# A macaron block with a selective scan on one core: the product of dt and u made by VectorE, two units later, in place of GpSimd

## What is computed

```python
x = x + 0.5 * ffn(layernorm(x))
x = x + attn(layernorm(x))          # its norm has a weight and a bias; attn adds its input too
x = x + 0.5 * ffn(layernorm(x))

# attn, per sequence: 512 channels d, 64 states s
x_ssm, z = split(h @ Win)
u  = silu(conv4(x_ssm) + conv_b)
dt = softplus(u @ dt_w + dt_b)
B, C = u @ Bp, u @ Cp
state = state * exp(dt * A) + (dt * u)[:, None] * B      # for each token in turn
y = einsum(state, C) + u * D
out = x + (y * silu(z)) @ Wout
```

## Time and profile before

| | |
|---|---|
| median of 3 runs | 5663.76 us (5656.84 to 5670.63) |
| profiled execution | 5668.32 us, its span 5666.1 us |
| granted TensorE clock | 0.972 of full speed |
| GpSimd busy | 5087.2 us, 90% of the span, 2326 instructions |
| VectorE busy | 5003.5 us, 88%, 4659 instructions |
| TensorE matmul busy | 4967.1 us, 88%, 85192 instructions |
| ScalarE busy | 3993.9 us, 70% |

### The profile page before, as it was taken

The page is one execution under the profiler, slowest core; times in us unless marked ns, Lnnn a source line. Parts: engine busy times, 40 slices in busy tenths (PEclk is TensorE's granted clock), DMA queues, the critical chain, the costliest instruction groups (busy, mean ns, idle before and its releaser), DMA issues.

```text
span 5666.1 us, 203628 instructions
## 1 busy us (share of the span) xinstructions
PE 4967.1 (88%) x85192; PEld 3086.8 (54%) x85192; DVE 5003.5 (88%) x4659; ACT 3993.9 (70%) x6625; POOL 5087.2 (90%) x2326
## 2 busy tenths in 40 slices
PE   4798988989889898998989889898898989889887
PEld 1455555555555555555555555555555555555554
DVE  1699989899998999989989898998989999898996
ACT  3677776777767677686767777777776777767564
POOL 0699898999989899898998989999899998989996
PEclk9899999999999999999999999999999999999998
DMA  5475565656547565565655656565475655646553
GB/s 159 146 172 189 152 182 173 168 191 157 188 162 176 181 167 184 164 173 181 169 189 152 180 180 170 188 167 186 159 178 184 172 187 158 180 169 176 193 181 114
DMA packets 578970, 977.29 MB, mean 172 GB/s; under 512 B 294881, under 2 KB 328450, under 8 KB 510466
## 3 DMA queue, kind: packets, MB, share of 16 engines
q1 hardware_dynamic: 313858, 961.82, 54.5%
q10 hardware_dynamic: 264192, 2.11, 3.0%
HBM read 875.74 MB, written 88.08 MB: 170 GB/s over the span
## 4 chain that ended last, share of the span: by engine, by line
POOL 57%; issue 25%; PE 10%; DVE 3%; DMA 2%; ACT 1%; POOLq 1%; ACTq 0%; DVEq 0%; SPq 0%
POOL H L625 54%; PE pUB L701 3%; PE Y L727 3%; DVE H L586 2%; PE pP L664 1%; POOL lnv L639 1%; DMA Bd<-scratch_diag 1%; POOL dto L643 1%; PE pP L658 1%; DMA Cb<-scratch_c 1%; PE pA L743 0%; POOLq L624 0%; DVE cv L537 0%; POOL X L649 0%; PE pA L741 0%
## 5 line engine op out<-in xcount | busy, mean ns | idle before, releaser
L625 POOL TENSOR_TENSOR H<-H,Cb 128x1024 f32<-128x1024 f32 x2048 | 4801.9, 2393 | 351.7 <-DVE H L586 344.9
L586 DVE TENSOR_TENSOR_SCAN H<-dA,pUB 128x512 f32<-128x512 f32 x4096 | 4678.6, 1202 | 464.2 <-PE pUB L701 438.0
L427 ACT ACTIVATE dA<-DT,w_negA 128x512 f32<-128x512 f32 x4096 | 2620.3, 711 | 1316.0 <-DVE H L586 1311.9
L701 PEld LDWEIGHTS pUB<-Bd,UT 64*64 64x64 f32 x65536 | 1963.9, 135 | 1427.1 <-issue 1416.8
L701 PE MATMUL pUB<-Bd,UT 64*64 64x128 f32 x65536 | 2282.6, 276 | 487.5 <-DVE H L586 405.0
L727 PE MATMUL Y<-H,w_ident 64*64 64x512 f32 x16384 | 2037.2, 607 | 93.0 <-POOL H L625 92.0
L727 PEld LDWEIGHTS Y<-H,w_ident 64*64 64x64 f32 x16384 | 670.6, 137 | 679.9 <-issue 668.9
L427 ACT ACT_TABLE_LOAD x224 | 287.4, 1283 | 4.0
L658 PE MATMUL pP<-hT,w_Win 128*128 128x512 f32 x512 | 266.3, 644 | 25.7 <-ACT uto L415 15.0
L664 PE MATMUL pP<-U,w_dt_w 128*128 128x512 f32 x512 | 259.2, 631 | 4.6 <-ACT zo L379 4.6
L639 POOL TENSOR_TENSOR lnv<-lnv,ev 128x512 f32<-128x512 f32 x64 | 81.2, 1269 | 82.3 <-DVE ev L600 82.3
(11 more groups left out here) (78 smaller groups left out, 1909.5 us busy)
## 6 DMA issues: line engine op xcount, KB each, us to landing
Cb<-scratch_c SPq DMA_DIRECT2D x512, 1024.0 KB, 5.3
Bd<-scratch_diag SPq DMA_DIRECT2D x512, 512.0 KB, 4.5
scratch_diag<-H SPq DMA_DIRECT2D x16, 1024.0 KB, 18.0
scratch_z<-zo SPq DMA_DIRECT2D x64, 256.0 KB, 6.1
scratch_dt<-dto SPq DMA_DIRECT2D x64, 256.0 KB, 5.8
scratch_ut<-uto SPq DMA_DIRECT2D x64, 256.0 KB, 6.3
DT<-scratch_dt SPq DMA_DIRECT2D x64, 256.0 KB, 4.9
UT<-scratch_ut SPq DMA_DIRECT2D x64, 256.0 KB, 5.6
```

What stands on the lines that cost most here:

```text
L427: last = nc.scalar.activation(dA[:, n % DAR, j, :], DT[:, k, :], ACT.Exp, scale=c["negA"][:, k, GS * blk + j:GS * blk + j + 1])
L586: last = nc.vector.tensor_tensor_scan(H[:, n % HR, 2 * i + j, :], dA[:, n % DAR, 2 * i + j, :], pUB[:, i, :].rearrange("p (t s) -> p s t", ...
L625: nc.gpsimd.tensor_tensor(h[:, j:j + 2, :], h[:, j:j + 2, :], Cb[:, blk % 2, j:j + 2, :], ALU.mult).then_inc(times_c, 1)
L701: last = nc.tensor.matmul(out, UT[rows, k, j * P + h * HP:j * P + h * HP + HP], Bd[rows, blk % 2, i, j * P:(j + 1) * P].rearrange("p (t s) ...
```

## The change

The product leaves GpSimd's dt step and becomes an instruction of VectorE behind its scans of unit 32, 37, 44 and 51, two units after the GpSimd additions of the same tile (behind unit 30, 35, 42, 49). VectorE waits for dto and for duo to be free. Nothing else is moved: the store of dto, the transposition and the tables of the other engines are as before.

```diff
-DVES = {..., "soft": (30, 35, 42, 49),
+DVES = {..., "soft": (30, 35, 42, 49), "du": (32, 37, 44, 51),
...
 # VectorE, behind the scans of unit n
+                    if proj and n in when["du"]:
+                        m = when["du"].index(n)
+                        s = KI * q + m
+                        dve.wait_ge(dt_done, at(s + 1))
+                        dve.wait_ge(mm_ut, at(s))
+                        nc.vector.tensor_tensor(duo[:, :], dto[:, :], U[:, m, :], ALU.mult).then_inc(du_done, 1)
...
 # GpSimd, behind its products of unit n
                         nc.gpsimd.tensor_tensor(dto[:, :], lnv[:, :], relu[:, :], ALU.add).then_inc(dt_done, 1)
-                        pool.wait_ge(dt_done, at(s + 1))
-                        pool.wait_ge(mm_ut, at(s))
-                        nc.gpsimd.tensor_tensor(duo[:, :], dto[:, :], U[:, m, :], ALU.mult).then_inc(du_done, 1)
```

More of the change, by code:

```diff
@@ L36 @@
         "turn 1": (18, 21), "turn c": (35, 37), "turn 3": (58, 60)}
-DVES = {"norm 1": (4,), "norm c": (21,), "norm 2": (40,), "norm 3": (52,), "soft": (30, 35, 42, 49),
+DVES = {"norm 1": (4,), "norm c": (21,), "norm 2": (40,), "norm 3": (52,), "soft": (30, 35, 42, 49), "du": (32, 37, 44, 51),
         "conv": (2, 6, 10, 14), "x2": (11, 15), "x1": (27, 32), "out": (42, 46)}
```

## The result

| | before | changed |
|---|---|---|
| median of 20 runs each | 5658.6 us (5638.8 to 5675.9) | 5674.5 us (5662.4 to 5690.3) |
| ratio | | 1.0025, 95% interval 1.0014 to 1.0035 |
| profiled execution's span | 5666.1 us | 5660.5 us |
| GpSimd busy, instructions | 5087.2 us, 2326 | 5032.8 us, 2262 |
| VectorE busy, instructions | 5003.5 us, 4659 | 5068.1 us, 4723 |

In this measurement the change costs a quarter of a percent; the forecast was 28 us less. The profiled execution of the changed kernel is the quickest of its 20 and that of before lies above its median, so the two spans say nothing of the sign. They can be compared place by place.

What follows compares the result with a forecast made beforehand. Any of GpSimd, VectorE and TensorE can bound a unit, with TensorE waiting for GpSimd behind dt steps. Gains of 1.8 us x 15 passes, 27 us, plus about 1 for q = 0, gave 5636 us; range 5595 to 5695.

Steps and rivals of the forecast that it cites:

- The port: SBUF port shared by VectorE and GpSimd: new product put at 0.67 us if free, 4 us or more if not.
- Case (b): VectorE waits only for GpSimd's running product, then goes ahead of the next; seen at 2101.09, L600 taking 2.17 us.
- (c): VectorE waits for the running GpSimd product and the whole next one; seen at unit 49, L600 taking 3.96 us.
- Rivals 1 and 2: VectorE let in after a queued product (+24 us, 5688, chance 0.14), or only when GpSimd runs dry (+122, 5785, 0.08).
- Unit 30: Product made behind unit 32: unit 33 starts 0.75 us later, taken up by about 0.8 us of slack; sum 0.
- Unit 35: Product made behind unit 37: GpSimd gains 1.35 us and pays 0.45, so all behind moves 0.9 us earlier.
- Unit 42: Product made behind unit 44: GpSimd gains 1.35 us less 0.45, 0.9, whether or not VectorE gets the product boundary.
- Unit 49: Product made behind unit 51: 0.67 us within 0.65 us of VectorE idling; sum 0, L600 still colliding.
- rival 4: More gain than forecast, as L600 at unit 49 takes 1.65 us rather than 3.96: 35 us more, 5601, chance 0.10.
- The sum: All four sites: 0 + 0.9 + 0.9 + 0 = 1.8 us a pass, 27 us over 15 passes.
- four rivals: Late at the port (0.14), never between two products (0.08), nothing measurable (0.18), more gain than thought (0.10).
- A: Experiments' theory, not forecast: gain is there, but TensorE runs out of fetched program where diagonal stores fill the DMA engines.

Runs made afterwards that it cites:

- e4: Changed kernel with four of the eight diagonal stores of B moved from units 32-35 to 40, 41, 43, 44; 0.9914 of before.
- e11: Same kernel as e4 (changed, four stores moved), run in one group with e9 and e10; 0.9886 of before, 5641.3 us.
- e5: Kernel before (product on GpSimd) with the same four stores moved to units 40, 41, 43, 44; 0.9979 of before.
- e10: Same kernel as e5 (before, four stores moved), run in one group with e9 and e11; 0.9917 of before, 5659.3 us.
- e1: The changed kernel run again without edit, for a second trace; 0.9991 of before.
- e9: The changed kernel once more, in one group with e10 and e11; 0.9998 of before, 5705.8 us.
- e2: Changed kernel, but the product of unit 30's tile stays on GpSimd; 0.9964 of before.
- e3: Against the kernel before, only the product of unit 30's tile goes to VectorE; 1.0035 of before.
- e8: Changed kernel with unit 30's product kept on GpSimd and four stores moved to units 40, 41, 43, 44; 0.9905 of before.
- e12: As e8, but the four stores spread to units 39, 44, 47, 55; 0.9865 of before, 5632.4 us.
- e6: Changed kernel with the load of C for unit 36 issued one GpSimd product later; 0.9988 of before.
- e7: Changed kernel with the product of unit 30's tile cut to one column; 0.9969 of before.

## Why the prediction was wrong

**What bounds the kernel**: three engines in turn, and TensorE's waits for GpSimd behind the dt steps as the thing to be won. Right as far as it went: of the 92.0 us, 37.7 went.

**The port**: right in what it forecast, not in its reason. Case (b) holds in the new places. The new product was put at 2.8, 1.2, 0.7 and 0.67 us; it takes 2.80 to 2.89 behind unit 32 in 14 of 15 passes, 0.67 to 1.29 behind unit 37 in 14, 0.67 to 0.73 behind 44 in 14, 0.67 behind 51 in 11. Rivals 1 and 2 fell here: no queued product went ahead, or it would have taken 5 us. The Trainium skill's exclusive lock (SBUF — State Buffer, section "SBUF: two separate sides") is what these places show: VectorE waited for the end of the running product, no longer. At unit 49 the trace still goes beyond it. The prediction took (b) rather than (c) because GpSimd's products overlap little there. That holds in the kernel before: at unit 49 VectorE was passed over in the 13 passes with overlaps of 0.08 us or more, and not in the two with 0.05. In the changed kernel it was passed over in 11 of 15 passes, four of them with overlaps of 0.03 to 0.06 us, no more than in the new places. One of the four, with the products around it, which start 2.32 us apart and last 2.36:

```profile
3535.30 3.99 DVE L600 SCALAR_TENSOR_TENSOR ev<-ev,absv 128x512 f32<-128x512 f32 x1
```

```profile
L631 POOL TENSOR_TENSOR H<-H,Cb x5: 2348/2356/2372, 3527.1 to 3536.4; 128x1024 f32<-128x1024 f32 x5
```

So the overlap doesn't decide it, and that (b) came out was in part luck. What does decide stays open.

**Unit 30**: unit 33 was to start 0.75 us later, counted from L600 of unit 30. That lies at 3084.9 in the changed kernel (its neighbour on GpSimd at 3085.09, 0.16 behind it as at 3106.11 in the earlier trace rows), so unit 33 starts 13.0 us behind it against 12.3 before: 0.7. "Sum: 0" is right where the pauses are gone (22.56 us in e4 and 22.63 in e11, against 22.77 and 22.63 in e5 and e10) and wrong by +2.8 us in the changed kernel. **This is the step that failed.** It let TensorE start whenever its inputs were ready, "as TensorE would allow", and never asked where its instructions come from. The rows to ask with were there: TensorE had 63.1 us of "issue" ahead of line 701 in the kernel before, though only 5.2 us of it are pauses in units 29 to 40. What the runs show in its place: the wait of 1.54 us goes, the piece that TensorE needs in unit 35 starts 6.4 us behind the end of the former one rather than 3.4 and takes 2.1 us rather than 0.9, and TensorE stands still for 1.35 to 3.33 us in each of 13 passes. With the stores moved (e4) 1.7 us of such pauses are left of 50.3. Why the fetch collides with the stores once the wait is gone is argued, not shown: in none of the 14 passes of the kernel before was a piece under way during that wait, so it isn't that TensorE stood still while the piece came.

**Unit 35**: 0.9 forecast, 0.64 measured over 36 to 42, 0.56 between e5 and e4, and 0.94 between e10 and e11. Right, if a little large.

**Unit 42**: 0.9 forecast, 0.93 measured. Right, and VectorE did get its boundary.

**Unit 49**: 0 forecast. 49 to 63 is 0.62 us shorter in the first trace, 0.06 in e1. L600 there gets in at the end of the running product (1.63 us) in two passes of the changed kernel in which it took 3.96 and 4.00 before, a touch of rival 4.

**The sum**: -1.8 a pass forecast, 27 us. With the stores moved the change is worth 18 us in the pair of one group (e10, e11), 37 by the pair across groups (e5, e4): the sum lies between, and its size is known no better than that. In the changed kernel as it is, +2.83 us at unit 35 eats it. None of the four rivals had this mechanism. That the range held the time is luck: it reached so far up for the sake of rival 1, which didn't come.

**What stays open.** The first measurement gave 1.0025, e1 0.9991, e9 0.9998: the changed kernel is slower in the first and level in the two groups in which before was 5706. By A the kernel before would lose time to pauses in the slower groups too, and e10's gain of 46 us points that way; no trace of before from them was taken. In the first trace of before there is little to gain there: units 33 to 36 take 23.04 us and 22.63 in e10, some 6 us in 15 passes. And TensorE's pause in unit 0 of a pass is there in 7 of 14 passes of before (16.8 us), in 8 to 10 of e2, e3, e8, e10 and e12, 5 of e5, but in none or one of changed, e1, e4, e6, e9, e11, and 3 of e7: it all but goes where VectorE makes all four products. It isn't what e11 gains on e10, whose trace has 23.4 us of it: up to unit 29 e11's pass is no shorter (160.36 us against 160.02, from the last scan of the former pass). TensorE's instructions are the same in all; I can't say why.

## What to carry to other kernels

Taking a wait out of an engine's way shifts it against everything else that runs: before you sum up what the removal gives, look at what that engine needs next, its own instruction fetch included. Here "issue" pauses came at the same matmul in every pass, inside a group that has no wait; that pointed to the ends of program pieces, and the stores in many tiny pieces nearby were the thing to move: worth 0.2 to 0.8% even without the change. The arithmetic of the shared port came out of the rows to a tenth of a microsecond, though not who goes first; when it gives zero for one site of several, leave that site alone. And run the two kernels that you compare on one chip: the same kernel before took 5659 to 5708 us from group to group.

## What the hardware showed that was not expected

Of the changed kernel's 711, the 47 that ran beside more than 300 packets of the 8-byte stores took 1.30 us at the median and up to 3.04; but full engines need not be the stores' doing: in the kernel before the longest piece, 3.19 us, ran beside none of them. TensorE goes on 1.3 to 2.7 us after the piece has landed (passes 1 to 13 of the changed kernel).
- VectorE's product with both inputs in SBUF waits for GpSimd's running product even if it is one column wide: 2.16 to 2.36 us for 128x1 (e7).
- Whether VectorE gets in between two queued products of GpSimd isn't told by how much they overlap: in all new places, with overlaps of 0.03 to 0.08 us, it did; at unit 49 of the changed kernel it was passed over in 11 of 15 passes, with overlaps of 0.03 to 0.12 us, and took 3.95 to 3.99 us there.
